# First softmax's exponentials, attended values and output projection as products of f16 halves

## The reference, cut to what matters

```python
x = x + layernorm(attn(layernorm(x)))        # x: 16 x 1024 x 256, float32
x = x + layernorm(ffn(layernorm(x)))
# attn: 16 heads of 16 channels, 64 landmarks
kernel1 = softmax(Q @ K_l.T)                 # 1024 x 64, the "first softmax"
kernel2 = softmax(Q_l @ K_l.T)               # 64 x 64, inverted by iteration (six steps)
kernel3 = softmax(Q_l @ K.T)                 # 64 x 1024
SV  = (kernel1 @ inv(kernel2)) @ (kernel3 @ V)
out = SV @ w_proj                            # 256 x 256
# ffn: eight experts are tried, the one of least reconstruction loss is used for the sequence
```

## Time and profile before

| | us |
|---|---|
| median of three runs | 2277.98 (2277.91 to 2283.66) |
| the profiled execution's own time | 2281.05 |
| its span, first to last instruction | 2279.3 |
| busy: PE | 2019.9 (89%) |
| busy: DVE | 1471.1 (65%) |
| busy: ACT | 864.9 (38%) |
| busy: POOL | 700.9 (31%) |
| mean granted TensorE clock, share of full | 0.964 |

### The profile page before, as it was taken

The page is one execution under the profiler, slowest core; times in us unless marked ns, Lnnn a source line. Parts: engine busy times, 40 slices in busy tenths (PEclk is TensorE's granted clock), DMA queues, the critical chain, the costliest instruction groups (busy, mean ns, idle before and its releaser), DMA issues.

```text
span 2279.3 us, 58742 instructions
## 1 busy us (share of the span) xinstructions
PE 2019.9 (89%) x24991; PEld 1307.2 (57%) x24991; DVE 1471.1 (65%) x3319; ACT 864.9 (38%) x1509; POOL 700.9 (31%) x916
## 2 busy tenths in 40 slices
PE   3888989999898998989899898989989898998945
PEld 1554747556474755647465564746657475665724
DVE  3667576766757667675766757576675757767531
ACT  3334344343433443343343434334343443334320
POOL 4153152322315232232523224251331424223051
PEclk9889999999999999999999999999999999999978
DMA  6213141221514222151422215132231513213020
GB/s 152 46 47 76 30 122 39 81 61 30 121 30 116 44 73 61 29 131 30 112 44 71 66 30 131 30 99 52 63 79 30 129 31 89 62 41 83 11 56 19
DMA packets 232972, 150.71 MB, mean 66 GB/s; under 512 B 153035, under 2 KB 203732, under 8 KB 232693
## 3 DMA queue, kind: packets, MB, share of 16 engines
q1 hardware_dynamic: 232710, 146.95, 27.5%
HBM read 36.98 MB, written 16.78 MB: 24 GB/s over the span
## 4 chain that ended last, share of the span: by engine, by line
PE 62%; DVE 17%; SPq 9%; issue 4%; ACT 3%; POOL 3%; DMA 2%; DVEq 1%; POOLq 0%; ACTq 0%
PE NS L979 11%; PE ringF L1187 9%; SPq L429 9%; PE ringF L1172 6%; PE KV L1060 5%; PE ringA L1146 5%; PE ringA L880 5%; PE ringF L1220 3%; PE ringA L1046 3%; PE ringA L1022 3%; DVE stage L1608 3%; DVE mx L1518 2%; PE ringF L880 2%; PE ringF L1222 2%; ACT E L690 2%
## 5 line engine op out<-in xcount | busy, mean ns | idle before, releaser
L1187 PE MATMUL ringF<-x,H 128*128 128x256 f16 x1536 | 237.9, 273 | 0.0
L1532 DVE TENSOR_REDUCE mx<-ringA 128x8 f32<-128x512 f32 x256 | 175.4, 685 | 89.3 <-PE ringA L1022 88.8
L682 ACT ACTIVATE E<-ringA,score_scale 128x512 f32<-128x512 f32 x256 | 175.5, 686 | 116.8 <-PE ringA L1046 116.7
L1187 PE MATMUL ringF<-H 128*128 128x128 f16 x1024 | 204.4, 220 | 1.4 <-DVE H L1619 1.4
L880 PE MATMUL ringA<-xT,wqkv 128*128 128x512 f16 x768 | 184.0, 391 | 21.2 <-ACT QS L700 11.7
L1585 DVE SCALAR_TENSOR_TENSOR X<-X,NS 128x320 f32<-128x320 f32 x160 | 78.0, 488 | 182.8 <-PE NS L979 177.7
L1518 DVE TENSOR_REDUCE mx<-ringA 128x1 f32<-128x512 f32 x256 | 160.1, 682 | 52.0 <-PE ringA L1013 51.5
L1172 PE MATMUL ringF<-wd,x2T 128*128 128x512 f16 x768 | 187.9, 384 | 6.4 <-DVE H L1619 3.1
L516 POOL TENSOR_SCALAR vtmp<-mv,eps_ffn 128x8 f32<-128x8 f32 x16 | 5.1, 316 | 612.0 <-DVE mv L1363 612.0
L690 ACT ACTIVATE E<-ringA,score_scale 128x512 f32<-128x512 f32 x256 | 158.6, 684 | 75.2 <-PE ringA L1077 75.2
L516 POOL TENSOR_SCALAR vtmp<-mv,eps_ln 128x8 f32<-128x8 f32 x32 | 9.9, 310 | 538.2 <-DVE mv L1363 538.2
(11 more groups left out here) (261 smaller groups left out, 4317.8 us busy)
## 6 DMA issues: line engine op xcount, KB each, us to landing
KS<-stage SPq DMA_DIRECT2D x384, 64.0 KB, 2.0
QS<-stage SPq DMA_DIRECT2D x384, 64.0 KB, 2.0
xin<-in_L_attn_x_dram SPq DMA_DIRECT2D x16, 1024.0 KB, 11.0
xres<-in_L_attn_x_dram SPq DMA_DIRECT2D x16, 1024.0 KB, 8.1
out_dram<-yout SPq DMA_DIRECT2D x16, 1024.0 KB, 5.5
QS<-LB SPq DMA_DIRECT2D x16, 512.0 KB, 4.4
E<-in_L_attn_w_qkv_dram SPq DMA_DIRECT2D x1, 768.0 KB, 7.0
H<-in_L_ffn_Wd_dram SPq DMA_DIRECT2D x2, 256.0 KB
```

The source lines that it names most:

```text
L682: A(E[:, k % ESLOTS, :], ps[:, :], ACT.Exp, scale=score_scale[:, 0:1]).then_inc(freed["s3"].sem, 1)
L1187: ins = MM(dst, H[:, a, t, own], src, start=first and i == 0, stop=last and i >= 3, skip_group_check=True)
L1532: V_.reduce_max(mx1[:, t, 8 * h:8 * h + 8], take(b, "m1", k)[:, :].rearrange("p (a m) -> p a m", a=8), AX.X)\
```

## The change

The exponentials of the first softmax, Y, the attended values and `w_proj` are kept as two f16 halves each, and the products with them are sums of f16 products: two passes for the sums, three for `attend` and the output projection. `E1` is the memory of `E` seen as two f16 halves per slot. ACT now computes each exponential twice, once to the f16 high half and once in float32 to `E1f`, which has two buffers. The low half is the difference: POOL makes it for pieces 0 to 11 (`LOWS = 12`), DVE for pieces 12 to 15. The attended values are made in float32 in `xsv` (the memory of `xtmp`), ACT copies the high half to `stage` (`attended_hi`), DVE subtracts for the low half (`attended_lo`). On POOL the twelve differences stand after `norm1(b + 1)` and before `ffn_residual(b - 1)` or, in batch 0, `ffn_weights`, which now splits `w_proj` too. Y is scaled by 0.25, and the epsilon of the layer norm behind it follows.

```diff
-        svT = stage[:, :, :, :].rearrange("p a b n -> p (a b n)").bitcast(F32).rearrange("p (k n) -> p k n", k=KC)
+        xsv = xtmp[:, :, :].rearrange("p t c -> p (t c)").rearrange("p (i n) -> p i n", i=2)
+        E1 = E[:, :, :].bitcast(F16).rearrange("p k (a n) -> p k a n", a=2)
+        E1f = sb("E1f", [P, 2, HALF])
...
+            def exponentials1_lo(b):                    # POOL
+                for k in range(LOWS):
+                    pool.wait_ge(freed["s1"].sem, freed["s1"].at(b, k + 1))
+                    pool.sem_inc(s_apart, 1)
+                    pool.tensor_tensor(E1[:, k % ESLOTS, 1, :], E1f[:, k % 2, :], E1[:, k % ESLOTS, 0, :], ALU.subtract).then_inc(e1_lo.sem, 1)
...
                 if more:
                     norm1(b + 1)
+                exponentials1_lo(b)
                 if first(b):
                     ffn_weights()
...
+                if k >= LOWS + 2:                       # ACT, exp1
+                    act.wait_ge(e1_lo2.sem, e1_lo2.at(b, k - LOWS - 1))
+                elif k >= 2:
+                    act.wait_ge(e1_lo.sem, e1_lo.at(b, k - 1))
...
-                A(E[:, k % ESLOTS, :], ps[:, :], ACT.Exp, scale=score_scale[:, 0:1]).then_inc(freed["s1"].sem, 1)
+                A(E1[:, k % ESLOTS, 0, :], ps[:, :], ACT.Exp, scale=score_scale[:, 0:1])
+                A(E1f[:, k % 2, :], ps[:, :], ACT.Exp, scale=score_scale[:, 0:1]).then_inc(freed["s1"].sem, 1)
+
+            def attended_hi(b, i):
+                act.wait_ge(freed["sv"].sem, freed["sv"].at(b, i + 1))
+                A(stage[:, i % 2, 0, (i // 2) * HALF:(i // 2 + 1) * HALF], xsv[:, i % 2, :], ACT.Copy).then_inc(sv_hi.sem, 1)
...
                 for k in range(ESLOTS, 2 * ESLOTS):     # ACT, body
                     exp1(b, k)
-                attn_out(b, (0, 1))
+                    if k in (9, 11):
+                        attended_hi(b, (k - 9) // 2)
+                attended_hi(b, 2)
+                attn_out(b, (0,))
+                attended_hi(b, 3)
+                attn_out(b, (1,))
...
-            def tiled(dst, left, i):
-                for j in range(GP):
-                    ins = MM(dst[32 * j:32 * j + 32, :], left(j), E[:, (GP * i + j) % ESLOTS, :], start=True, stop=True)
+            def tiled(dst, passes, left, i):
+                for n, (a, c) in enumerate(passes):
+                    for j in range(GP):
+                        ins = MM(dst[32 * j:32 * j + 32, :], left(a, j), E1[:, (GP * i + j) % ESLOTS, c, :],
+                                 start=n == 0, stop=n == len(passes) - 1)
...
-                pe.wait_ge(freed["s1"].sem, freed["s1"].at(b, GP * (i + 1)))
+                if i < LOWS // GP:
+                    pe.wait_ge(e1_lo.sem, e1_lo.at(b, GP * (i + 1)))
+                else:
+                    pe.wait_ge(e1_lo2.sem, e1_lo2.at(b, GP * (i + 1) - LOWS))
...
                     if k % 2 == 0:                      # PE, output_projection
-                        pe.wait_ge(freed["sv"].sem, freed["sv"].at(b, 2 + k))
+                        pe.wait_ge(sv_lo.sem, sv_lo.at(b, 2 + k))
...
-                        for kc in range(KC):
-                            ins = MM(ps[:, i * C:(i + 1) * C], svT[:, kc, t * P:(t + 1) * P], wproj[:, kc, :],
-                                     start=kc == 0, stop=kc == KC - 1)
+                        ins = three(ps[:, i * C:(i + 1) * C], lambda a, kc: stage[:, kc, a, t * P:(t + 1) * P],
+                                    lambda a, kc: wproj[:, a, kc, :])
...
-                output_projection(b, (0, 1))
+                output_projection(b, (0,))
                 attend(b, 3)
+                output_projection(b, (1,))
...
-                    V_.tensor_tensor(Yblk[0:M, :, 0:D], ps[0:M], bcast(cinv[0:M, :], D), ALU.mult)
-                    V_.tensor_tensor(Yblk[M:P, :, D:2 * D], ps[M:P], bcast(cinv[M:P, :], D), ALU.mult)\
-                        .then_inc(th_done.sem, 1)
+                    Yf = Z[:, 0, :, :]
+                    V_.scalar_tensor_tensor(out=Yf, in0=ps, scalar=SVS, in1=bcast(cinv[:, :], D),
+                                            op0=ALU.mult, op1=ALU.mult).then_inc(y_step.sem, 1)
+                    dve.wait_ge(y_step.sem, y_step.at(b, 1))
...                                                       # two copies to the high half, two differences
...
-                for i in range(2):                      # DVE, body
-                    attended(b, i)
-                for part in range(2):
-                    invert_sums(b, 2, part)
+                attended(b, 0)
+                attended(b, 1)
+                attended_lo(b, 0)
+                attended_lo(b, 1)
+                exponentials1_lo(b, 12)
+                invert_sums(b, 2, 0, more)
+                exponentials1_lo(b, 13)
+                invert_sums(b, 2, 1, more)
+                exponentials1_lo(b, 14)
+                exponentials1_lo(b, 15)
                 attended(b, 2)
-                for part in range(2):
-                    invert_sums(b, 3, part)
+                invert_sums(b, 3, 0, more)
+                attended_lo(b, 2)
+                invert_sums(b, 3, 1, more)
                 attended(b, 3)
+                attended_lo(b, 3)
```

More of the change, by code:

```diff
@@ L1125, in sum_exponentials @@
                     pe.wait_ge(freed["sv"].sem, freed["sv"].at(b, 2))
-                done(tiled(bank("ss", i), lambda j: sel32[:, :], i), "ss")
+                done(tiled(bank("ss", i), ((0, 0), (0, 1)), lambda a, j: sel16[:, :], i), "ss")
             def attend(b, i):
@@ L1135, in attend @@
                     pe.wait_ge(freed["ss"].sem, freed["ss"].at(b, 3))
-                done(tiled(bank("sv", i), lambda j: Yblk[:, (i % 2) * GP + j, :], i), "sv")
+                done(tiled(bank("sv", i), PASSES, lambda a, j: Yblk[:, a, (i % 2) * GP + j, :], i), "sv")
             def output_projection(b, ks):
                 for k in ks:
+                    if k == 0 and first(b):
+                        pe.wait_ge(s_setp.sem, POOL_PROJ)
                     if k % 2 == 0:
-                        pe.wait_ge(freed["sv"].sem, freed["sv"].at(b, 2 + k))
+                        pe.wait_ge(sv_lo.sem, sv_lo.at(b, 2 + k))
                     ps = get(b, "pr", k)
@@ L1598, in thin, with invert_sums @@
                 else:
[L1599 to L1605 removed]
+                    Yf = Z[:, 0, :, :]
+                    V_.scalar_tensor_tensor(out=Yf, in0=ps, scalar=SVS, in1=bcast(cinv[:, :], D),
+                                            op0=ALU.mult, op1=ALU.mult).then_inc(y_step.sem, 1)
+                    dve.wait_ge(y_step.sem, y_step.at(b, 1))
+                    for e in range(2):
+                        rows, cols = slice(e * M, (e + 1) * M), slice(e * D, (e + 1) * D)
+                        ins = V_.tensor_copy(Yblk[rows, 0, :, cols], Yf[rows, :, :])
+                    ins.then_inc(y_step.sem, 1)
+                    dve.wait_ge(y_step.sem, y_step.at(b, 2))
+                    for e in range(2):
+                        rows, cols = slice(e * M, (e + 1) * M), slice(e * D, (e + 1) * D)
+                        ins = V_.tensor_tensor(Yblk[rows, 1, :, cols], Yf[rows, :, :], Yblk[rows, 0, :, cols], ALU.subtract)
+                    ins.then_inc(th_done.sem, 1)
+            def invert_sums(b, i, part, more):
+                cols = slice(part * HALF // 2, (part + 1) * HALF // 2)
                 if part == 0:
+                    if i == 0 and more:
+                        dve.wait_ge(xlo.sem, xlo.at(b + 1, 2))
+                    if i >= 2:
+                        dve.wait_ge(sv_lo.sem, sv_lo.at(b, i - 1))
                     dve.wait_ge(full["ss"].sem, full["ss"].at(b, i + 1))
[L1608 removed]
+                ins = V_.reciprocal(xsv[:, i % 2, cols], bank("ss", i)[:, cols])
                 if part:
```

87 lines of the change are left out of this document (56 added, 31 removed).

## The result

| | before | after |
|---|---|---|
| median of the runs, us (before: all runs to that point) | 2277.94 | 2470.48 (2464.88 to 2478.72) |
| ratio | | 1.0854 [1.0822, 1.0886] |
| the profiled execution, its span | 2281.05, 2279.3 | 2464.88, 2463.2 |
| mean granted clock | 0.964 | 0.932 |

The kernel became 8.5% slower, 193 us by the medians; the forecast was 171 us. The profiled execution is the fastest of the four after, so that its span grew by 9 less than the medians did. To see where the 183.9 us of span went, I cut every batch at three marks on PE: the first product of the iteration, attend 0, and the end of the last output projection. "Front" is from there to the next batch's first mark.

The account below looks back on a forecast made before the run. The tail was taken as PE's, with DVE's chain binding after the change: 16 x (10.2 + 0.5) + 11 = 182 us, rounded down to 171; 2278 + 171 = 2449 us, eight-tenths range 2385 to 2500.

Parts of the forecast that it names:

- the walk: Tail, step by step along ACT's and DVE's work: last projection ends at 119.3, not 112.6, so the tail grows 6.7 us.
- Contention in the tail: DVE's two-input differences wait for whole POOL instructions in the tail: 2.3 us a batch, between zero and 4 with the iteration.
- The clock: Tail: PE, idle longer, runs sums 3, projection 0 and attend 3 at half clock; +8.1 in place of +6.7 without contention.
- PE's own end: Tail: with the clock's fall and no contention, PE itself finishes at 120.7.
- The iteration: Before the tail: DVE's `G`, on the chain to the adapter, meets POOL's differences 4 and 5; 0.5 us a batch.
- Batch 0: POOL's `ffn_weights` starts later and is 3.4 us longer, delaying the attention's norm: 11 us once, at least 6.
- PE's busy time: Sign on the profile page: PE's busy time lower by 50 to 80 us.
- PE-bound: Rival, tail: ACT's and DVE's additions lie beside PE, 4 us less in 16 tails; 2214 us, 5%.
- Only ACT binds: Rival, tail: DVE's differences fall into its waits and +4 a batch remains; 2348 us, 7%.
- Clock without contention: Rival, tail: PE's clock falls but POOL's and DVE's instructions seldom meet, +8.1 a batch; 2419 us, 18%.
- no contention, no fall of the clock: Rival, tail: only the walk's +6.7 a batch, plus 11 for batch 0; 2396 us, 12%.
- the signs that I named: Checks: tail 26 to 27.5 us, clock below 0.9, slow DVE differences, reciprocals 1.7, ACT up 190, last-projection-to-DMA stretch unchanged, larger batch 0.

Follow-up runs that it names:

- the later `wup`: Changed kernel with the last two steps of POOL's ffn_weights in batch 0 moved behind attn_residual(0) and norm2(0): 2461.27 us, 1.0812.
- the memset kernel: Changed kernel with POOL's differences 0 to 7 replaced by memsets of the low half to zero: 2433.4 us, 1.0682.

## Why the prediction was right, and where a size was off

**DVE's serial chain is the floor: shown.** From attend 0 the walk had low 15 done after 14.3 us; it took 14.25. Attended 3 was due after 19.7 and came after 20.2. Taking four differences away from it (sixteen on POOL) shortened the tail by 2.4 us, 1.4 of them by the chain itself, and making them small let sums 3 begin 1.7 us sooner.

**Contention in the tail: right in kind, too large.** I took 2.3 us. The parts that I named, 0.3 for low 12, 0.3 to 0.5 each for low 13 to 15 and 2 for one difference beside an addition, make 3.2 to 3.8 and not the 2.5 to 3.5 that I wrote. Low 12, 13 and 15 took 0.63 to 0.68 and low 14 took 0.77: together they lost 0.15 beside the norms. There it was POOL that waited (its norms 5.28 for 4.31, and 1.27 for a 0.32 operation). On the chain only the last difference paid much, 1.3 in batch 13. The low halves of attended 0 and 1, for which I had no term, took 1.33 each beside POOL's differences 8 to 11; but DVE had to wait for exponential 12 until 8.1 us after attend 0 in any case, so that they cost at most 0.1. Making POOL's work small gave back 1.5, splitting the additions 1.3.

**The clock: right in kind, +0.5 on the chain and not +1.4.** Sums 3 at 1.04 for 0.61 made the reciprocal wait 0.62, where with the clock held it waits 0.19. Projection 0 at half clock (2.58) is off the chain, since DVE's second reciprocals were late anyway, and PE's own end, which I had at 120.7, was not what decided. (The durations that I gave add up to 120.1 for it; I showed no working.) The walk of 6.7, with 0.5 for the clock, 1.3 for the last difference and 0.3 of small starts, makes the 8.8 measured, where I had 10.2. The last two effects do not simply add: without POOL's additions the tail is 1.5 shorter, with the clock held up to attended 3 DVE's last difference ends only 0.1 sooner.

**The iteration: mis-sized.** I took 0.5 us, measured is 1.1 in eight batches and 2.8 in seven. Two `G` of batch 13 take 1.37 and 1.43 for 0.69; and the copy of `dsel`, for which I had no term:

```profile
L1738 DVE COPY dsel<-wdown x16: 227/605/610, 288.6 to 2428.0; 128x256 f16 x16
```

0.23 before, 0.61 now. The 1.7 us between the two kinds of batch is the adapter at half clock in some batches, behind the wait for `bsel` that has grown from 0.63 to 2.18 us; it never appears where useless matmuls fill that wait. I had looked for the clock's fall in the tail only. With batch 0's this term is worth 31 us for the 8 I gave it, and the memset kernel removes it all. It cancels the other error: the tails have 140 us for 16 x 10.2 = 163. That the sum came near is in part luck. My sum before rounding was 182, nearer to what was measured than the 171 that I went by; I had rounded the contention down.

**Batch 0: right.** 11 us forecast, 9.4 measured, 8.4 of them gone with the later `wup`.

**PE's busy time: wrong.** I expected 50 to 80 us less; it fell by 3.7. Full-clock durations were nearly right (0.83 for attend where I had 0.75, 0.61 for sums where I had 0.53, 1.48 for a projection). But in one tail the half clock adds, against these, 0.4 for sums 2, 0.4 for the scores behind them, 0.5 for attend 2, 0.4 for sums 3 and 1.1 for projection 0, 2.8 us; 45 us in 16 batches, and 12 more in seven adapters. Busy time is no measure of work when the clock moves.

The rivals: *PE-bound* fell, since PE idles 10 of 26 us. *Only ACT binds* fell with the sixteen differences on POOL, where ACT has the same work and the tail shrinks, and with the second exponential made small, which left sums 3 where they were. *Clock without contention* (2419) fell with the additions split, worth 31 us, and with it *no contention, no fall of the clock* (2396), as the clock was 0.60 while sums 3 ran. Of the signs that I named, the tail (25.8) lies just below 26 to 27.5; its clock (0.87), the differences (mean 1.02, the longest 2.52), the reciprocals (1.75), ACT (+185), the fronts (+1.6 in sum) and the larger growth of batch 0 are as written, and PE's busy time is not. The sum by measured terms: 140 in the tails, 31 in the iterations, 9.4 for the front of batch 0 and 3.0 elsewhere make 184 of 184.

## What to carry to other kernels

Swapping float32 products for halves moves work from PE to the engines that make the halves: walk those engines' serial chain through the stretch before counting what PE saves. Here the saving alone, without the differences, was 0.9%, and the differences cost ten times that. Keep a long GpSimd instruction with SBUF inputs away from a VectorE one with two of them, or cut it in pieces; splitting two 1024-column additions gave 31 us. And after any edit look again at who meets whom: several of the edits here won time where they were made and lost it where a chain met POOL at another phase, where PE then idled long enough to run at half clock, or where SP's transfers came late.

## What the runs showed of the hardware that was not expected

- A DVE difference that began inside a POOL addition of 1024 columns ended 0.55 us behind it. One that began 0.43 us into the first of two back-to-back additions took 4.77 us, until both were done, in three batches, and 2.46 us, getting in between the two, in others of the same kernel. In another kernel one that began 0.20 us ahead of the first took 5.40. One of 0.69 us can so cost as much as two POOL instructions.
- The reverse holds for small ones: POOL's 128 x 8 operation behind the differences took 1.27 us in 15 of 16 batches, 0.31 when alone.
- A DVE f16 copy with one SBUF input went from 0.23 to 0.61 us beside POOL's differences and to 0.30 beside its memsets, while reciprocals from PSUM stayed at 1.75.
- PE at half clock followed waits of 2.1 to 3.7 us in several places, but the wait alone does not decide. The adapter waited 2.18 us in every batch of the changed kernel and ran at half clock in seven. The same 24 matmuls took 2.79 us after a wait of 2.15, 4.43 after one of 2.38 and 5.17 after one of 3.69; the first two are neighbouring batches of one kernel.
- SP's second transfer of a staging, issued 0.6 us behind the first in the changed kernel, came some 3 us behind it in most batches when a store and two loads of 1 MB had been issued just before.
